# Expert products of a decoder layer as three fp32r products of halves, with the halves made early and read back in a ring

## What is computed

```python
gate = xt @ Wr + br
_, ids = jax.lax.top_k(gate + gate_bias, TOPK)          # TOPK = 2 of 7
masked = ...                                            # gate at ids, -inf elsewhere
probs = jax.nn.softmax(masked, axis=-1)
u = jnp.einsum('nh,ehi->eni', xt, Wup) + bup[:, None, :]
g = jax.nn.silu(jnp.einsum('eni,eij->enj', u, Wgate) + bgate[:, None, :]) * u
eo = jnp.einsum('enj,ejh->enh', g, Wdown) + bdown[:, None, :]
out = jnp.einsum('ne,enh->nh', probs, eo)
su = xt @ Wsu + bsu                                     # the shared expert: the same with its own weights
out = out + (jax.nn.silu(su @ Wsg + bsg) * su) @ Wsd + bsd
```

## Time and profile before

| | us |
|---|---|
| median of 3 runs | 2395.71 |
| lowest and highest | 2387.66, 2403.41 |
| the profiled execution, its own time | 2405.38 |
| its span | 2403.5 |
| PE busy | 2201.0 (92%) |
| DVE busy | 1782.6 (74%) |
| ACT busy | 1517.6 (63%) |
| POOL busy | 785.2 (33%) |

### The profile page before, as it was taken

One profiled execution on the slowest core, in us unless ns is written; L12 is line 12 of the kernel. 1 busy time (PEld: TensorE's weight loads), 2 busy tenths in 40 slices (PEclk: granted clock), 3 DMA queues, 4 the chain that ended last, 5 costly groups with the idle time before them and its releaser, 6 DMA issues.

```text
span 2403.5 us, 47902 instructions
## 1 busy us (share of the span) xinstructions
PE 2201.0 (92%) x17852; PEld 1763.1 (73%) x17852; DVE 1782.6 (74%) x3472; ACT 1517.6 (63%) x3517; POOL 785.2 (33%) x672
## 2 busy tenths in 40 slices
PE   5569999999999999999999999999996899999998
PEld 4458888888888888888888888888884455455555
DVE  5889897787979888797988879797435755556543
ACT  4446766756676766667677676765665667565632
POOL 1533543434344444434444353333222100100000
PEclk8779999999999999999999999999998999999999
DMA  3322223212231322223122321312113000000000
GB/s 74 86 71 56 76 48 71 61 44 63 50 82 40 71 55 60 63 46 85 31 77 52 66 63 44 76 21 54 28 21 105 1 1 1 10 1 10 1 9 9
DMA packets 262340, 113.22 MB, mean 47 GB/s; under 512 B 208328, under 2 KB 239584, under 8 KB 262112
## 3 DMA queue, kind: packets, MB, share of 16 engines
q1 hardware_dynamic: 262112, 110.17, 19.3%
HBM read 82.58 MB, written 27.53 MB: 46 GB/s over the span
## 4 chain that ended last, share of the span: by engine, by line
issue 43%; POOL 25%; PE 23%; DVE 7%; ACT 1%; SPq 1%; DMA 1%; POOLq 0%; DVEq 0%; ACTq 0%
POOL EB L423 5%; POOL SM L497 5%; PE ps L1546 5%; PE ps L1538 4%; PE ps L1555 4%; POOL SM L504 3%; POOL EB L427 3%; POOL SZ L499 3%; POOL Q L475 2%; POOL WL L406 2%; PE ps L1478 2%; PE ps L1469 2%; PE ps L1488 1%; DVE A L783 1%; PE ps L1494 1%
## 5 line engine op out<-in xcount | busy, mean ns | idle before, releaser
L783 DVE SCALAR_TENSOR_TENSOR A<-ps,CW,A 128x508 f32<-128x508 f32 (+2 forms) x768 | 516.3, 734 | 128.4 <-ACT A L576 121.9
L492 POOL TENSOR_SCALAR SM<-SM 128x8 f32<-128x8 f32 x64 | 12.6, 197 | 917.4 <-ACT DL L595 917.4
L1198 PE MATMUL ps<-XH,WH 128*128 128x512 f32 x512 | 227.1, 443 | 50.8 <-DVE A L783 47.3
L1326 PE MATMUL ps<-WO,DL 128*128 128x256 f32 x1024 | 242.7, 391 | 0.2 <-ACT TTF L692 0.2
L1326 PEld LDWEIGHTS ps<-WO,DL 128*128 128x128 f32 x1024 | 192.3, 193 | 29.4 <-ACT DL L582 0.8
L1200 PE MATMUL ps<-XH,WL 128*128 128x512 f32 x512 | 211.5, 413 | 0.0
L1199 PE MATMUL ps<-XL,WH 128*128 128x512 f32 x512 | 211.0, 412 | 0.0
L735 ACT ACTIVATE SC<-ps,A 128x128 f32<-128x128 f32 x512 | 140.6, 389 | 111.0 <-DVE A L1108 110.0
L595 ACT ACTIVATE DL<-SZ 128x128 f32<-128x128 f32 x512 | 152.2, 298 | 76.3 <-issue 46.8
L1000 DVE TENSOR_TENSOR SZ<-SZ,ps 128x512 f32<-128x512 f32 x128 | 86.4, 686 | 131.4 <-PE ps L1352 131.4
L985 DVE TENSOR_TENSOR BP<-ps,EB 128x512 f32<-128x512 f32 x256 | 158.6, 681 | 16.3 <-PE ps L1417 13.7
(11 more groups left out here) (212 smaller groups left out, 5535.4 us busy)
## 6 DMA issues: line engine op xcount, KB each, us to landing
EB<-decay_rows SPq DMA_DIRECT2D x128, 256.0 KB, 4.6
x_blocks<-BP SPq DMA_DIRECT2D x256, 32.0 KB, 1.6
X<-x_blocks SPq DMA_DIRECT2D x16, 512.0 KB, 6.2
...
TTF<-tt_blocks SPq DMA_DIRECT2D x256, 32.0 KB, 1.9
...
```

What stands on the lines that cost most here:

```text
L783: dve.scalar_tensor_tensor(acc, ps(i, 0, [[128, 4], [1, 128 - s]]), at(CW, tile * 4 + 3 - s, [[1, 1]]), acc, ALU.mult, ALU.add).then_inc(s ...
L1198: pe.matmul(out, sa, ma, start=(kt == 0), stop=False)
L1326: t = pe.matmul(ps(7 - i, b * 256, [[1, 256]]), at(DL, (4 * i + 2 * b + v) * 128, [[1, 128]]), at(WO, (k // 4 % 2) * 512 + v * 256, [[1, 2 ...
```

## The change

The up and gate products are computed as three fp32r products. For this, both operands are split. **The weights** are split once, on the chip, in ticks 2 to 7: SP loads an expert's up and gate weights (`load_raw`), ACT writes high halves (`split_raw_hi`), POOL low halves (`split_raw_lo`), and SP stores both to DRAM, 1 MB per expert (`store_halves`). SPLITS says which experts a tick takes: one in ticks 2, 3, 6 and 7, two in ticks 4 and 5. **In the blocks** SP reads an expert's halves back into a ring of four, and its down weights into a ring of two, for each of the 32 pairs of group and expert. **Activations:** the router's step r0 makes an exact copy in WO, a high half on ACT and a low half on POOL. After an up step ACT writes the high half of u with its bias, DVE the low half from the same bank (which frees the bank), and POOL adds the two to u, which the gate multiplication reads. The orders of all engines are written anew; down products stay fp32. SBUF is laid out anew for this, and a few semaphores are joined; none of that adds an instruction.

```diff
-XB, UB, SB = 4096, 16384, 17408
+HL = 16384
+SPLITS = {2: (0,), 3: (1,), 4: (2, 3), 5: (4, 5), 6: (6,), 7: (7,)}
...
-PE_ORDER = ("s0 s1 s2 T1 ua0 w0 n ua1 w1 r3 ub0 r0 s3 s4 s5 r4 ub1 ga0 w3 w4 ga1 s6 s7 w2 gb0 gb1 r1 "
-            "v0 w5 w6 da0 w7 da1 t0 db0 v1 db1")
...
+PE_ORDER = ("s0 s1 s2 T1 ua0 w0 n ua1 w1 ub0 r0 s3 s5 s4 r3 ub1 r4 ga0 w3 w4 ga1 s6 s7 w2 gb0 gb1 r1 v0 da0 w5 w6 "
+            "t0 da1 db0 w7 db1 v1")
...
-POOL_STEPS = list(mixed_steps("n X1", "n X1", "X1 n f0 f1"))
+POOL_STEPS = list(mixed_steps("n X1", "n X1 r0",
+                              "X1 ua0 ua1 ub0 n r0 ub1 f0 f1"))
...
+        def raw(e8, off=0, n=1024):
+            return at((VV, DL)[e8 % 2], off, [[1, n]])
+        def halves(e8, off, n):
+            return at((BP, SZ)[e8 % 2], HL * (1 - e8 % 2) + off, [[1, n]])
...
-        def we(e8, part):
+        def we(idx, part, off, n):
+            return at(WE, (idx % 4) * 2048 + part * 512 + off, [[1, n]])
+        def w_down(idx, off, n):
+            return at(EB, 2048 + (idx % 2) * 512 + off, [[1, n]])
...
+                def load_raw(e8):
+                    if e8 >= 2:
+                        sp.wait_ge(sem["raw_lo"], 2 * (e8 - 2) + 2)
+                    elif e8:
+                        sp.wait_ge(sem["hj"], 2)
+                    for part, w in enumerate((wsu, wsg) if e8 == 7 else (wup[e8], wgate[e8])):
+                        sp.dma_start(at((VV, DL)[e8 % 2], part * 512, [[256, 2], [1, 256]]),
+                                     w.rearrange("(k p) n -> p k n", p=128)).then_inc(ld_raw[e8 % 2], 16)
+                def store_halves(e8):
+                    sp.wait_ge(sem["raw_lo"], 2 * e8 + 2)
+                    sp.dma_start(hl_scr[e8], halves(e8, 0, 2048)).then_inc(st_hl[e8 % 2], 16)
...
+                    if n == 0:
+                        load_raw(1)
+                    for e8 in SPLITS.get(n, ()):
+                        store_halves(e8)
+                        if e8 + 2 < 8:
+                            load_raw(e8 + 2)
...
-                for e8 in range(8):
-                    for part, (routed, shared) in enumerate(((wup, wsu), (wgate, wsg), (wdown, wsd))):
-                        src = shared if e8 == 7 else routed[e8]
-                        sp.dma_start(at(BP, we(e8, part), [[256, 2], [1, 256]]),
-                                     src.rearrange("(k p) n -> p k n", p=128)).then_inc(sem_e[e8], 16)
-                for b in range(B):
+                for j in range(2):
+                    sp.wait_ge(st_hl[j], 64)
+                for idx in range(32):
+                    e8 = idx % 8
+                    if idx >= 12 and idx % 8 == 4:
+                        for b in range(idx // 2 - 6, idx // 2 - 2):
+                            sp.wait_ge(sem["x3"], b + 1)
+                            sp.dma_start(out[b], y_row(b)).then_inc(sem["st_out"], 16)
+                    if idx >= 4:
+                        sp.wait_ge(sem["gate"], 2 * (idx - 4) + 2)
+                    sp.dma_start(at(WE, (idx % 4) * 2048, [[1, 2048]]).bitcast(f32), hl_scr[e8]).then_inc(sem_e[idx % 4], 16)
+                    if idx >= 2:
+                        sp.wait_ge(sem["down"], 2 * (idx - 2) + 2)
+                    sp.dma_start(w_down(idx, 0, 512).rearrange("p (k n) -> p k n", k=2),
+                                 (wsd if e8 == 7 else wdown[e8]).rearrange("(k p) n -> p k n", p=128)).then_inc(ld_down[idx % 2], 16)
+                for b in range(12, 16):
...
+                def split_raw_lo(e8):
+                    for part in range(2):
+                        pool.wait_ge(sem["raw_hi"], 2 * e8 + part + 1)
+                        pool.tensor_tensor(halves(e8, part * 1024 + 512, 512).bitcast(f32r), raw(e8, part * 512, 512),
+                                           halves(e8, part * 1024, 512), ALU.subtract).then_inc(sem["raw_lo"], 1)
...
+                    for e8 in SPLITS.get(n, ()):
+                        split_raw_lo(e8)
...
+                    elif kind == "r0":
+                        for kt in range(2):
+                            pool.wait_ge(sem["x2_hi"], 2 * a + kt + 1)
+                            if a >= 2:
+                                pool.wait_ge(sem["up"], 16 * (a - 1))
+                            elif a:
+                                pool.wait_ge(sem["o_mm"], 2 * NSTEP)
+                            pool.tensor_tensor(x2_lo(a, kt * 512, 512), at(WO, kt * 512, [[1, 512]]),
+                                               x2_hi(a, kt * 512, 512).bitcast(f32), ALU.subtract).then_inc(sem["x2_lo"], 1)
+                    elif kind == "u":
+                        pool.wait_ge(sem["u_lo"], 2 * a + i + 1)
+                        if a >= 2:
+                            pool.wait_ge(sem["glu"], 2 * (a - 2) + 2)
+                        pool.tensor_tensor(u_buf(a, i * 512, 512), u_hi(a, i * 512, 512).bitcast(f32),
+                                           u_lo(a, i * 512, 512).bitcast(f32), ALU.add).then_inc(sem["u"], 1)
...
+                    if m == 0 and i == 0:
+                        act.wait_ge(st_hl[1], 64)
...
+                def split_raw_hi(e8):
+                    act.wait_ge(ld_raw[e8 % 2], 32 * (e8 // 2 + 1))
+                    if e8 >= 2:
+                        act.wait_ge(st_hl[e8 % 2], 16 * (e8 // 2))
+                    elif e8:
+                        act.wait_ge(sem["hj"], 2)
+                    for part in range(2):
+                        act.activation(halves(e8, part * 1024, 512).bitcast(f32r), raw(e8, part * 512, 512), ACT.Copy).then_inc(sem["raw_hi"], 1)
...
+                    for e8 in SPLITS.get(n, ()):
+                        split_raw_hi(e8)
...
+                            if a:
+                                act.wait_ge(sem["gate_mm"], a)
+                                act.wait_ge(sem["x2_lo"], 2 * a)
+                            act.activation(at(WO, kt * 512, [[1, 512]]), ps(2 + kt), ACT.Copy).then_inc(sem["x2_T"], 1)
-                            act.activation(at(x2_buf(a), kt * 512, [[1, 512]]), ps(2 + kt), ACT.Copy).then_inc(sem["x2_T"], 1)
+                            act.activation(x2_hi(a, kt * 512, 512), ps(2 + kt), ACT.Copy).then_inc(sem["x2_hi"], 1)
...
-                            act.wait_ge(sem["glu"], 2 * (a - 2) + 2)
+                            act.wait_ge(sem["gate"], 2 * (a - 2) + 2)
+                            act.wait_ge(sem["u"], 2 * (a - 2) + 2)
-                        act.activation(u_buf(a, i * 512, [[1, 512]]), ps(i), ACT.Identity,
-                                       bias=q(Q_BUP + 8 * i + a % 8, [[1, 1]])).then_inc(sem["u"], 1)
+                        act.activation(u_hi(a, i * 512, 512), ps(i), ACT.Identity,
+                                       bias=q(Q_BUP + 8 * i + a % 8, [[1, 1]])).then_inc(sem["u_hi"], 1)
-                        act.activation(s_buf(a, i * 512, [[1, 512]]), ps(2 + i), ACT.Silu,
+                        act.activation(s_buf(a, i * 512, 512), ps(2 + i), ACT.Silu,
...
+                    if n == SLOTS - 1:
+                        dve.wait_ge(st_hl[0], 64)
...
+                    elif kind == "u":
+                        dve.wait_ge(sem["u_hi"], 2 * a + i + 1)
+                        dve.scalar_tensor_tensor(u_lo(a, i * 512, 512), ps(i), q(Q_BUP + 8 * i + a % 8, [[1, 1]]),
+                                                 u_hi(a, i * 512, 512).bitcast(f32), ALU.add, ALU.subtract).then_inc(sem["u_lo"], 1)
-                        s_ap = s_buf(a, i * 512, [[1, 512]])
+                        s_ap = s_buf(a, i * 512, 512)
-                        dve.tensor_tensor(s_ap, s_ap, u_buf(a, i * 512, [[1, 512]]), ALU.mult).then_inc(sem["glu"], 1)
+                        dve.wait_ge(sem["u"], 2 * a + i + 1)
+                        dve.tensor_tensor(s_ap, s_ap, u_buf(a, i * 512, 512), ALU.mult).then_inc(sem["glu"], 1)
...
-                            free[2 + kt] = sem["x2_T"], 2 * a + kt + 1
+                            free[2 + kt] = sem["x2_hi"], 2 * a + kt + 1
-                                t = pe.matmul(ps(1, b * 8, [[1, 7]]), at(x2_buf(a), kt * 512 + b * 128, [[1, 128]]),
+                                t = pe.matmul(ps(1, b * 8, [[1, 7]]), at(WO, kt * 512 + b * 128, [[1, 128]]),
...
-                        pe.wait_ge(sem["x2_T"], 2 * g + 2)
-                        pe.wait_ge(sem_e[e8], 48)
+                        pe.wait_ge(sem["x2_hi"], 2 * g + 2)
+                        pe.wait_ge(sem["x2_lo"], 2 * g + 2)
+                        pe.wait_ge(sem_e[a % 4], 16 * (a // 4 + 1))
-                            t = pe.matmul(ps(i), at(BP, we(e8, 0) + kt * 256 + i * 128, [[1, 128]]), at(x2_buf(g), kt * 512, [[1, 512]]),
-                                          start=(kt == 0), stop=(kt == 1))
+                            w = kt * 256 + i * 128
+                            t = three(ps(i), we(a, 0, w, 128), we(a, 1, w, 128), x2_hi(g, kt * 512, 512), x2_lo(g, kt * 512, 512), kt)
-                        free[i] = sem["u"], 2 * a + i + 1
```

(12 more changed lines are left out.)

97 lines of the change are left out of this document (56 added, 41 removed).

## The result

The changed kernel took 2411.76 us (median of 11 runs, 2398.55 to 2424.69), the kernel before in the same session 2390.75 (11 runs, 2376.63 to 2407.38): a ratio of 1.0076, 95% interval 1.0039 to 1.0114. By the ratio it is slower by some 18 us (the interval is 9 to 27 us), where 12 less were forecast. The profiled execution took 2424.69 us with a span of 2423.0; against the span before, 2403.5, that is 19.5 more.

The account below looks back on a forecast made before the run. DVE and its feeding chain were taken to bound ticks 5 and 6, PE the later ticks and expert blocks. Experts -22 and early ticks +9.5 gave -12: 2384 us against 2395.71, range 2358 to 2406.

Parts of the forecast that it names:

- The splits in ticks 2 to 7: Early ticks: copies and subtractions lengthen the loop through a tick, delaying the DVE chain by 6.5 us (3 to 9).
- The slots themselves: Early ticks: ACT's copies and POOL's subtractions for the splits, +9.5 us as 6.5 of delay plus 3 at the port.
- The port term: Ticks 5 to 7: DVE products of two SBUF tensors slow beside eight POOL subtractions, 3 us (0 to 10).
- rival 3: Port in full: eight subtractions cost DVE 10.2 us, not 3, and POOL's additions meet gate multiplications; 2391 us, chance 0.12.
- all but the first group have a block to hide them: Router's extra ACT copies and POOL subtractions: hidden by a block, the first group by s0 to T1; 0, at most +1.
- The products: Expert blocks: an up or gate step falls from 1.72 to 1.42 us, saving 2.4 us per block of eight steps.
- The waits: Attention blocks: ub0 waits 0.4 us and w4 0.8 for exponentials, taking 1.2 of the 2.4 us gain.
- Router, normalisation, ring: Router copies and 1.25 MB loads per expert: 0 taken, ends +1 us and up to 1 us per block; ring slack 6.3.
- The clock in the blocks: Expert blocks: waits of half a microsecond should not lower PE's clock from 1.00, its upper level of 2.4 GHz.
- 1: Products pay in full, with low halves ahead of every wait and early delay only 3 us; 2361 us, chance 0.20.
- 2: DVE keeps the banks: low halves 1 us later, four waits of 1 us per attention block; 2416 us, chance 0.10.
- 4: Ring late: the odd expert comes 2 us late in each of four experts-alone blocks, +8; 2392 us, chance 0.06.

Follow-up runs that it names:

- SP's order alone: Changed kernel with SP issuing the half stores and next raw loads ahead of the store of the tick's products, not behind it; ratio 0.9972 against the kernel before.

## Why the prediction was wrong

**The step that failed** is in "The splits in ticks 2 to 7": it built the new loop from ACT's copy, POOL's subtractions, the decay and the exponential, and gave the delay as 6.5 with bounds of 3 and 9. The raw loads and the 1 MB stores had neither a duration nor a place in SP's queue, though the change puts eight stores and six of the loads behind store_x and load_rows. kq_silu(5) came at 112.67 where 103 was forecast, and kq_tap3(6) at 134.91 where 113 was. SP's order alone was worth 19 us (185.7 to 166.5), two thirds of the way from the -12 that was forecast to the +18 that came. The trace of before has no such wait, but the latency stood in it: the earlier trace rows has 8.5 us for a load, which the text used for the ring and not here.

**The slots themselves** were right in kind and near in size: 9.5 forecast, 11.2 measured. The port term, 3 inside it, measured 3.9, but over the twelve subtractions from kq_silu(4) on, not the eight that it counted. The term of the whole of each subtraction (rival 3) is out. In the changed kernel itself none of it shows: over the same stretch DVE is busy for 61.72 of 94.40 us, before for 67.66 of 70.23.

**Run-up, forecast 0, came to +8.8.** 3.9 are the new orders, 3.3 of them w4 behind p0 to p2. The line "all but the first group have a block to hide them" looked at the copies for the router and not at what the last order does to DVE's queue. The other 4 or so go with TensorE's clock in that execution.

**The products.** A block of experts alone was put at 18.5 us and takes 18.40, with the 0.28 wait of ub0 that 1.6 against 1.42 gave. An attention block was put at 30.4 and takes 30.73. The term that was off is the lone step: between fp32 work a step takes 1.69, 1.49, 1.56 and 1.58 us from its start to the next, a pair 2.84 and 2.94: 12.10 for eight, 1.7 less than 8 x 1.72, not 2.4. The 0.05 per step that was left "in the range" is 0.09. The waits were right: 1.2 forecast; ub0 starts 0.73 behind w1 (2018.19) where the transpositions need 0.44, and w3 to ga1 takes 1.58 (2024.39 to 2025.97) where 0.88 were needed, 1.0 together. The first attention block gained nothing (34.46 against 34.40): the clock was at 0.95 in it.

**Router, normalisation, ring: 0** held. An expert's 1 MB landed in 5.0 us (median of 32 loads), inside the slack of 6.3, and PE's waits name no load. **The clock in the blocks** stayed at 1.00 in the plain ones, as said.

**The rivals.** 1 is out: gains of 0.76 and 2.24 per block, not 2.4 and more. 2 is out: the eight waits of PE for low halves add to 3.1 us over all blocks, the longest 1.1. 3 is out for the early ticks as said above; what POOL's additions do to the gate multiplications in the blocks no run isolates, but a plain block was only 0.33 us above the forecast. 4 is out by the waits of PE. None of the five cases held the cause, and the chance of 0.06 for slower by over 1% was drawn from a rival that had nothing to do with it.
